# One transpose issued a tile later, and a one-column silu behind the last gelu of each pair, in a fused two-block kernel

## What is computed

```
h = layernorm(x) * (1 + ca) + sa
x = x + ga * (layernorm(ssm(h Wp + bp) Wo + bo + h) * gamma + beta)    # block 0, state space
h = layernorm(x) * (1 + cb) + sb
h = silu(h w1) * (h w2);  h = gelu(h h1);  h = gelu(h h2)               # block 0, FFN
x = x + gb * (h w3)
...                                                                     # block 1: gated linear attention, LoRA FFN
```

## Time and profile before

| | |
|---|---|
| median of three runs | 574.4 us |
| the profiled execution | 574.15 us |
| its span | 572.3 us |
| TensorE, products | 535.9 us busy, 94% |
| VectorE | 392.2 us, 69% |
| ScalarE | 346.3 us, 61% |
| GpSimd | 195.9 us, 34% |
| mean granted clock of TensorE | 0.979 |

### The profile page before, as it was taken

One profiled execution on the slowest core, in us unless ns is written; L12 is line 12 of the kernel. 1 busy time (PEld: TensorE's weight loads), 2 busy tenths in 40 slices (PEclk: granted clock), 3 DMA queues, 4 the chain that ended last, 5 costly groups with the idle time before them and its releaser, 6 DMA issues.

```text
span 572.3 us, 10235 instructions
## 1 busy us (share of the span) xinstructions
PE 535.9 (94%) x3768; PEld 442.0 (77%) x3768; DVE 392.2 (69%) x1019; ACT 346.3 (61%) x629; POOL 195.9 (34%) x261
## 2 busy tenths in 40 slices
PE   8599988998999999989999999999999969999995
PEld 6558866875787688778787878888888858888884
DVE  5986978695869675559676777777777854645433
ACT  3878868767776789375555554645555424465541
POOL 3401530222011021033472727273737342534311
PEclk8889999999999999989999999999999989999998
DMA  8500000000005000000000000000000000000001
GB/s 303 147 2 1 1 0 1 1 2 1 1 1 179 1 1 2 0 1 2 1 1 2 1 1 1 1 3 1 1 1 3 1 0 1 21 19 19 28 29 38
DMA packets 10821, 11.72 MB, mean 20 GB/s; under 512 B 753, under 2 KB 9393, under 8 KB 10641
## 3 DMA queue, kind: packets, MB, share of 16 engines
q1 hardware_dynamic: 9712, 10.50, 5.6%
q10 hardware_dynamic: 1056, 0.52, 0.3%
HBM read 8.92 MB, written 2.10 MB: 19 GB/s over the span
## 4 chain that ended last, share of the span: by engine, by line
PE 50%; ACT 3%; DVE 3%; issue 1%; DVEq 0%; ACTq 0%
PE bank L1934 10%; PE bank L2014 6%; PE bank L167 6%; PE bank L169 5%; PE bank L168 5%; PE bank L1926 3%; PE bank L1947 3%; PE bank L1981 3%; PE bank L1969 2%; PE bank L2006 1%; PE bank L1956 1%; PE bank L243 1%; ACT att_qT L1745 1%; PE bank L2022 1%; PE bank L1920 1%; ACT h_hi L249 1%
## 5 line engine op out<-in xcount | busy, mean ns | idle before, releaser
L1072 PE MATMUL bank<-ffn_g_hi,w_hi 128*128 128x512 f32 x288 | 116.9, 406 | 0.1
L1073 PE MATMUL bank<-ffn_g_lo,w_hi 128*128 128x512 f32 x288 | 114.1, 396 | 0.0
L1415 DVE TENSOR_TENSOR_SCAN att_decay<-bank,norm_out 128x512 f32<-128x512 f32 x64 | 77.6, 1213 | 34.4 <-PE bank L1926 34.4
L611 DVE TENSOR_TENSOR ffn_g_lo<-ffn_full,ffn_g_hi 128x512 fp32r<-128x512 f32 x96 | 67.1, 698 | 27.3 <-ACT ffn_full L857 25.9
L1934 PEld LDWEIGHTS bank<-att_qT,h_full 128*128 128x128 f32 x512 | 66.8, 193 | 5.3 <-issue 1.6
L1934 PE MATMUL bank<-att_qT,h_full 128*128 128x128 f32 x512 | 68.8, 278 | 0.2 <-DVE att_outer L1447 0.2
L1072 PEld LDWEIGHTS bank<-ffn_g_hi,w_hi 128*128 128x128 f32 x288 | 54.3, 188 | 13.9 <-issue 1.7
L1779 ACT COPY att_qT<-bank 128x512 f32<-128x512 f32 x64 | 37.3, 587 | 44.5 <-PE bank L169 41.1
L1073 PEld LDWEIGHTS bank<-ffn_g_lo,w_hi 128*128 128x128 f32 x288 | 54.4, 189 | 11.6
L1423 DVE TENSOR_TENSOR att_prob<-bank,att_decay 128x512 f32<-128x512 f32 x64 | 42.7, 667 | 21.1 <-issue 16.5
L857 ACT ACTIVATE ffn_full<-bank,cols 128x512 f32<-128x512 f32 x64 | 44.2, 696 | 19.7 <-PE bank L1073 14.5
(11 more groups left out here) (242 smaller groups left out, 1228.6 us busy)
## 6 DMA issues: line engine op xcount, KB each, us to landing
out<-att_vw SPq DMA_DIRECT2D x7, 256.0 KB, 2.3
x<-in_x SPq DMA_DIRECT2D x3, 512.0 KB, 11.6
w_raw<-in_w_all SPq DMA_DIRECT2D x1, 1152.0 KB, 8.4
w_raw<-in_w_all SPq DMA_DIRECT2D x1, 768.0 KB, 9.7
stage<-in_sel SPq DMA_DIRECT2D x1, 640.0 KB, 8.3
v_raw<-in_v_all SPq DMA_DIRECT2D x1, 576.0 KB, 5.8
x<-in_x ACTq DMA_DIRECT2D x2, 256.0 KB, 3.5
w_raw<-in_w_all SPq DMA_DIRECT2D x1, 512.0 KB, 4.8
```

The source lines that it names most:

```text
L611: dve.tensor_tensor(lo, full[j % 4][:, :], hi.bitcast(F32), ALU.subtract).then_inc(low, 1)
L1072: pe.matmul(acc, w[0], x[0], start=start, stop=False)
L1073: return pe.matmul(acc, w[0], x[1], start=False, stop=stop)
L1415: dve.tensor_tensor_scan(decay[at % ND][:, :], bank("decay", b, k)[:, :], ident4[:, :], 0.0, ALU.mult, ALU.add).then_inc(decay_ready, 1)
```

## The change

Two edits are made together. The first `flip_h` of a pair moves from behind tile 16 to behind tile 17 on TensorE, and the `bring_h` that copies it moves from behind gelu 17 to behind gelu 18 on ScalarE. This is done for pairs 0 and 1. The second edit adds one activation on ScalarE behind gelu 23 of pairs 0 to 2, ahead of `bring_y`. It takes the silu of one column of a constant and writes it to a place that nobody reads afterwards (`scT`, whose memory the first gelu layer's high parts also use).

```diff
@@ loop_uses
-                    if i < 2 and j == 16:
+                    if i < 2 and j == 17:
                         uses.append((("flip", 2 * i + 4), 6))
@@ ScalarE
-                            if j in (17, 22):
+                            if j in (18, 22):
                                 bring_h(e + 2 + (j == 22))
@@ ScalarE, behind the loop over j
+                    if i < 3:
+                        act.activation(scT[:, 0, 0:1], r["neg_half"][:, 0:1], ACT.Silu)
                     bring_y(2 * i)
```

## The result

The changed kernel took 569.83 us (median of five runs, 567.59 to 570.11), the kernel before 574.16 us in the five runs beside it (572.91 to 574.52). The ratio is 0.992, with a 95% interval from 0.9896 to 0.9945. The change saves 4.3 us (3.2 to 6.0 by the interval); 570.4 was forecast.

The account below looks back on a forecast made before the run. In the front, TensorE was taken to wait for ScalarE's silu, with the table load on the path between pairs. Gains of 1.43 + 1.43 + 1.16 = 4.02 us, the transpose move at 0, gave 570.4 us, range 568.9 to 572.5.

Parts of the forecast that it names:

- The table load is on the path between pairs: Between pairs, ScalarE idles 2.37 us, then loads the silu table only after y scaling; TensorE and VectorE wait for silu 0.
- Changes 1 and 2: First two switches between pairs of sequences: silu 0 starts 1.43 us earlier at each, with y scaling still on time.
- change 3: Third switch between pairs, with less idle cover: y scaling 0.27 us late, silu 0 still 1.16 us earlier.
- All of it is kept: After the first pair switch, VectorE's run is released by silu 2, so the whole first layer moves by 1.43 us.
- Rival A: At pair switches, only TensorE's idle 0.92 us each is saved, VectorE being full: 2.8 us in all; chance 0.12.
- Rival B: TensorE waits 1.4 us longer at the second transpose; only the third pair switch gains, 1.2 us; chance 0.08 including no effect.
- The drain: At ScalarE table switches, the skill page's extra 1380 ns was judged unseen; its figure would make the sum 1.6 us.
- rival C: A table switch behind a gelu takes 1.28 us longer than behind y scaling: 1.9 us gained in all; chance 0.05.
- Edit 2: First transpose and its copy a tile later in pairs 0 and 1: 0 us, bounds 1.5 lost to 0.6 gained.
- The second transpose's stop: TensorE's 3.3 us wait in two pairs stays, released by VectorE moments, GpSimd power and ScalarE normalise, behind VectorE's backlog.
- Rival D: Extra stretches of TensorE at 1.2 GHz after standstills, up to 1.7 us each, make it slower, 577.2 us; chance 0.04.
- The sum: Gains at the three pair switches, 1.43 + 1.43 + 1.16 = 4.02 us, with bounds from 2.8 to 4.3.

Follow-up runs that it names:

- e1: Kernel before plus the one-column silu alone, with the transpose and its copy left in place; 568.94 us, 0.9921 of the kernel before.
- e3: The full change with the one-column silu behind the scaling of y instead of ahead of it; 574.16 us, 1.0006 of the kernel before.
- e6: The full change with the one-column silu only at the third change of pair; 572.31 us, 0.9982 of the kernel before.
- e5: The full change with one-column silu, gelu and silu (three table loads) in place of the one silu; 578.29 us, 1.0107 of the kernel before.
- e2: Kernel before with only the first transpose and its copy moved a tile later, no extra silu; 573.41 us, 0.9997 of the kernel before.
- e10: The full change with the first transpose's copy directly behind gelu 19, ahead of normalise; 568.85 us, 0.9922 of the kernel before.
- e7: The full change with the first transpose's copy behind gelu 19, the FFN copy and normalise; 582.74 us, 1.0157 of the kernel before.
- e4: The full change with the second transpose of pairs 0 and 1 also a tile later on TensorE; 567.64 us, 0.9901 of the kernel before.
- e8: The full change plus a one-column gelu ahead of the last rounding of each pair's first layer; 568.81 us, 0.9923 of the kernel before.

## Why the prediction was right, point by point

- **The table load is on the path between pairs.** Shown by e1 and e3: the same load, in the idle time or behind it, makes the whole difference.
- **Changes 1 and 2, 1.43 each.** Silu 0 gained 1.42 at the first (5.06 to 3.64 behind the gelu). By e6 the two together are worth 2.90, 1.45 each. The small silu took 0.20, as taken. At change 3 the next activation starts 0.11 behind its start, where 0.13 was reckoned. From the first y scaling to the second there are 52.06 us (84.99 to 137.05), where 52.1 was forecast.
- **Change 3, 1.16.** Silu 0 gained 1.19, and alone this change shortens the front way by 1.15 (e6).
- **All of it is kept.** VectorE's run, released by silu 2, moved as a whole. Rival A, that VectorE keeps a part, would have given 2.8; 4.05 were measured. Rival B, that the gain is given back at the second transpose, would have left the stop in pair 1 1.4 longer; the stops are 1.53 and 1.76 us, where they were 1.54 and 1.76.
- **The drain.** In the changed kernel the load behind the wide gelu starts 0.02 us after the gelu's end and the small silu starts with the load's end (82.63, 82.65, 83.94), and in e5 three switches in a row came 1.50 us apart, small activation included. So rival C has no support here. The Trainium skill's page "ScalarE: Activation LUTs", section "What ACT_TABLE_LOAD costs", gives 1283 ns for the load and 2.66 us for a switch; every row of a load agrees with the first, and none with the second.
- **Edit 2 at nothing.** Right by e2. But the bound beside it, a loss of 0.77 in each pair if the copy came too late, was worked out the wrong way, and the runs depart from it on both sides. With a stop of 1.54 in each pair nothing was lost, since the next stop takes it up (e10). With the copy behind an instruction that itself waits, the front way grew by 14.6 (e7). A bound has to ask what is ahead in the queue and what stops next, and not how long the copy takes.
- **The second transpose's stop "sits behind VectorE's backlog".** The stop did stay in the full change, as forecast, and `normalise` is still released by GpSimd (L718); that VectorE's backlog is what sets its time was not tried. Yet its 3.3 us in the wait table were not what it costs: e4 took it away and won 1.19.
- **Rival D, the clock.** It did not decide the result. One low-clock stretch came and went between profiles, at the start of the second stage (see the last section). From pair 0's first gelu to the last pair's end the clock was full (1.00) in all profiles but those of e5 and e7, which make TensorE stop longer.
- **The sum** was 4.02 and the front way shows 4.05. The spans differ by 4.4. Of the rest, 0.28 lies ahead of pair 0's first gelu table load (46.24 us before, 45.96 after), and the change touches nothing that far forward. The forecast of 570.4 lies 0.6 above the median, within what the medians move by.

## What to carry to other kernels

In these runs moving an ACT_TABLE_LOAD paid only where an idle wait of ScalarE stood ahead of it and others waited behind it (e3, e8). There a one-column activation of the new function, put ahead of that wait, hides the switch of about 1.4 us as far as the idle time reaches: wholly with 2.37 us idle, and all but 0.24 us with 1.18 (rows of the third change). The scaling of y between the two brought no load of its own. When a stop on the busiest engine goes (e4), look for the next consumer of the same late data before counting it as won, and before an instruction is moved in a queue, look at what waits ahead of it there (e7).

## What the runs showed of the hardware that was not expected

The granted clock behind the same stop is not always the same. At the change of stage TensorE stands still for 2.03 us in every profile. Behind it the clock fell to 1.2 GHz for a stretch in nine of the twelve, and stayed at 2.4 GHz in three (e3, e6, e10). Here are the change (240 to 244) and e3 (244 to 248), where the second stage begins at 240.6 and 244.5:

```profile
240.00:244.00 4.00, 3.39 (x15) 3.23 (x16) 2.17 (x4) 3.08 (x6) 1.05 (x5) 0.66 0.00 0
```

```profile
244.00:248.00 4.00, 3.49 (x21) 3.17 (x22) 2.27 (x4) 3.17 (x6) 1.15 (x5) 1.00 0.00 0
```

Behind the stop, 3.4 us of the one hold 15 products and 3.5 us of the other 21. The second stage took 325.8, 326.5 and 325.8 us in the three without the fall, and 327.1 to 328.1 in the nine with it. The difference of 0.7 to 2.3 us is of the size by which runs of one kernel differ (572.91 to 574.52 us for the five runs of before), and a reason to judge changes of 1 us by a stretch of the trace as well as by the median.
